# Products of queries and keys laid out element by element for the sum on TensorE

## The reference

```
xn = layernorm(x)
q = xn @ Wq + bq                      # (B, T, 16 heads, 8)
kv = (xn @ Wdown + bdown) @ Wup + bup # (B, T, 16 heads, 16)
k, v = split(kv)
att = einsum('bthd,btgd->bthg', q, k) / sqrt(8)
att = softmax(att)
out = einsum('bthg,btgd->bthd', att, v) @ Wout + bout
x = x + out + moe0(xn)                # 8 experts, top 2
x = x + hyena(layernorm(x)) + moe1(layernorm(x))
```

## Time and profile before

| | us |
|---|---|
| median of 3 runs | 1367.02 |
| lowest and highest | 1363.98, 1368.1 |
| the profiled execution | 1364.03 |
| its span, first to last instruction | 1362.1 |
| TensorE matmuls busy | 1123.0 (82%) |
| VectorE busy | 831.2 (61%) |
| GpSimd busy | 796.9 (59%) |
| ScalarE busy | 596.3 (44%) |
| mean granted TensorE clock | 0.954 |

### The profile page before, as it was taken

How to read it: one execution, slowest core, us unless ns; L and a number is a source line. 1 busy time by engine, 2 the same in 40 slices (tenths; PEclk the granted TensorE clock), 3 DMA queues, 4 the chain that set the end, 5 groups by cost and what they waited for, 6 DMA issues and landing times.

```text
span 1362.1 us, 19492 instructions
## 1 busy us (share of the span) xinstructions
PE 1123.0 (82%) x6608; PEld 873.0 (64%) x6608; DVE 831.2 (61%) x1139; ACT 596.3 (44%) x1529; POOL 796.9 (59%) x613
## 2 busy tenths in 40 slices
PE   1448999999998988988783458899869999999975
PEld 1432222223887776777672457799868899899965
DVE  7946999997999999999998975111121000000038
ACT  0120011112766566656564448800005666656667
POOL 4605877873889899989881004767533445445520
PEclk9998999999999999999995779999989999999988
DMA  5471332131454554554445420199995767777747
GB/s 174 161 298 64 112 115 111 51 102 33 143 165 145 155 147 147 162 150 152 136 130 196 155 92 30 53 296 327 317 338 145 204 203 202 205 204 202 203 187 216
DMA packets 119955, 225.63 MB, mean 166 GB/s; under 512 B 16709, under 2 KB 80101, under 8 KB 117810
## 3 DMA queue, kind: packets, MB, share of 16 engines
q1 hardware_dynamic: 102164, 188.16, 44.9%
q0 software_dynamic: 17344, 35.57, 7.2%
q10 hardware_dynamic: 350, 0.67, 0.2%
HBM read 157.19 MB, written 67.14 MB: 165 GB/s over the span
## 4 chain that ended last, share of the span: by engine, by line
PE 42%; POOL 24%; DVE 11%; DMA 10%; ACT 6%; issue 6%; SPq 1%; POOLq 0%; ACTq 0%; DVEq 0%
PE ps L721 14%; POOL BG L259 12%; POOL y_tok L429 12%; PE ps L679 9%; PE ps L692 9%; DMA TPB<-in_kpad 5%; DVE XN L893 3%; DMA FF<-sorted_x 2%; PE ps L803 2%; DVE stats L863 2%; PE ps L805 2%; PE ps L668 1%; PE ps L730 1%; DMA xt_d<-xT 1%; DVE X L1037 1%
## 5 line engine op out<-in xcount | busy, mean ns | idle before, releaser
L429 POOL DMA_INDIRECT y_tok<-FF,yidx x284 | 306.9, 1081 | 206.0 <-ACT FF L497 146.0
L421 POOL DMA_INDIRECT sorted_x<-XN,idx x256 | 278.8, 1089 | 90.1 <-issue 89.0
L692 PE MATMUL ps<-FF 128*128 128x128 f32 x2272 | 278.8, 276 | 0.0
L692 PEld LDWEIGHTS ps<-FF 128*128 128x128 f32 x2272 | 266.9, 193 | 14.4 <-issue 4.3
L679 PE MATMUL ps<-FF 128*128 128x256 f32 x1136 | 273.8, 385 | 0.0
L488 ACT ACTIVATE FF<-ps,FF 128x256 f32<-128x256 f32 x568 | 230.2, 481 | 34.0 <-PE ps L679 33.1
L679 PEld LDWEIGHTS ps<-FF 128*128 128x128 f32 x1136 | 208.5, 194 | 23.3
L721 PE MATMUL ps<-BG,cst 128*128 128x512 f32 x208 | 193.3, 1097 | 0.0
L1146 DVE TENSOR_TENSOR BG<-BG,ps 128x512 f32<-128x512 f32 x16 | 10.6, 686 | 290.6 <-PE ps L837 290.4
L259 POOL TENSOR_TENSOR BG<-TPB 128x2048 f32<-128x2048 f32 x38 | 171.6, 4515 | 25.6 <-DVE BG L1028 13.6
L1016 DVE TENSOR_TENSOR BG<-BG,TPB 128x1024 f32<-128x1024 f32 x128 | 147.8, 1215 | 0.0
(11 more groups left out here) (185 smaller groups left out, 1676.7 us busy)
## 6 DMA issues: line engine op xcount, KB each, us to landing
FF<-in_moe SPq DMA_DIRECT2D x142, 514.0 KB
TPB<-in_kpad SPq DMA_DIRECT2D x22, 1024.0 KB, 7.8
sorted_x<-TPB SPq DMA_DIRECT2D x36, 516.0 KB, 4.1
FF<-sorted_x SPq DMA_DIRECT2D x142, 129.0 KB
FF<-in_kpad SPq DMA_DIRECT2D x10, 1024.0 KB
BG<-y_tok SPq DMA_DIRECT2D x8, 1024.0 KB, 6.6
X<-y_tok SPq DMA_DIRECT2D x8, 1024.0 KB, 6.5
y_tok<-FF,yidx POOLq DMA_INDIRECT x284, 3.2
```

The costliest lines, as they stand in the source:

```text
L421: pool.indirect_dma_start(sorted_x[layer], bass.IndirectOffsetOnAxis(ap=idx[:, k, j:j + 1], axis=0), XN[:, j, :], None).then_inc(s_sc, 16)
L429: pool.indirect_dma_start(y_d[layer], bass.IndirectOffsetOnAxis(ap=yidx[:, G % 4, r:r + 1], axis=0), ys[:, G % 4, r * D:(r + 1) * D], None ...
L692: t = pe.matmul(psY[:, r * P:(r + 1) * P], hT[:, G % 2, m, r * P:(r + 1) * P], wc[:, G % 4, HID + m * D:HID + (m + 1) * D], start=False, s ...
```

## The change

For the first 13 pairs the layout of `qkv` for queries and keys changes from head by head (16 heads of 8 elements) to element by element (8 elements, each with 16 heads). The evacuation on ScalarE, which was one copy of 384 columns, becomes a copy of 256 that regroups queries and keys as it reads them from PSUM, and a plain copy of 128 for the values. `own_product` on VectorE still takes 4 instructions of 1024 elements a pair, each over 4 elements, 16 heads and 16 heads. In them the query is repeated along the innermost dimension, and the key along the middle one. `prod` then holds, for each element, the 256 scores of a tile side by side. The matmuls of `sum_products` read two runs of 256 floats, one of each tile; their count, size and accumulation are the same. Pairs 13 to 31 keep their layout and their code, and no wait is added or removed.

```diff
@@ evac_qkv, ScalarE
-                act.copy(qkv[:, m % 4, t, :], bank[:, 0:3 * D]).then_inc(s_qkv, 1)
+                if m < OWN:
+                    act.copy(qkv[:, m % 4, t, 0:2 * D].rearrange("p (a e h) -> p a e h", a=2, e=DH),
+                             bank[:, 0:2 * D].rearrange("p (a h e) -> p a e h", a=2, e=DH))
+                    act.copy(qkv[:, m % 4, t, 2 * D:3 * D], bank[:, 2 * D:3 * D]).then_inc(s_qkv, 1)
+                else:
+                    act.copy(qkv[:, m % 4, t, :], bank[:, 0:3 * D]).then_inc(s_qkv, 1)
@@ sum_products, TensorE
-                pr = prod[:, b % 2, :].rearrange("p (n e) -> p e n", e=DH)
+                pr = prod[:, b % 2, :].rearrange("p (t e n) -> p e t n", t=2, e=DH)
                 for e in range(DH):
-                    t = pe.matmul(psS[b % 2][:, :], ident, pr[:, e, :], start=(e == 0), stop=(e == DH - 1))
+                    t = pe.matmul(psS[b % 2][:, :].rearrange("p (t n) -> p t n", t=2), ident, pr[:, e, :, :],
+                                  start=(e == 0), stop=(e == DH - 1))
@@ own_product, VectorE
                 dve.wait_ge(s_qkv, 2 * b + 2)
+                n = DH // 2
                 for t in range(2):
-                    for h0 in (0, H // 2):
-                        i = qk_product(dve, b, t, h0, H // 2)
+                    for e0 in (0, n):
+                        q = qkv[:, b % 4, t, e0 * H:(e0 + n) * H].rearrange("p (e h) -> p e h", e=n)
+                        k = qkv[:, b % 4, t, D + e0 * H:D + (e0 + n) * H].rearrange("p (e g) -> p e g", e=n)
+                        o = t * 2048 + e0 * H * H
+                        i = dve.tensor_tensor(
+                            prod[:, b % 2, o:o + n * H * H].rearrange("p (e h g) -> p e h g", e=n, h=H),
+                            q[:, :, :, None].to_broadcast([P, n, H, H]), k[:, :, None, :].to_broadcast([P, n, H, H]),
+                            ALU.mult)
```

## The result

The changed kernel took 1351.62 us (median of four, 1349.03 to 1351.73), the kernel before, timed beside it, 1365.5 us (1362.06 to 1368.1). The ratio is 0.9891, with a 95% interval of 0.9871 to 0.9912: 1.1% faster. The forecast was 1355.8 with 1351 to 1362. Applied to the 1367.02 us of before, the ratio gives 1352.1. The profiled execution took 1351.53 us, its span 1349.4, against 1364.03 and 1362.1.

The account below looks back on a forecast made before the run. TensorE's strided sum held back the first expert tile, with GpSimd's scatter and row loads next. First tile -12.6 us, cold start +1.4, sum -11.2 from 1367.02: 1355.8 us, range 1351 to 1362.

Parts of the forecast that it names:

- the stride is the price: On TensorE, line 721's read of every eighth float makes blocks slow; reading neighbours takes 6.9 us in place of 14.7.
- the steady step: VectorE's step falls from 17.98 to 16.42 us, with no wait for the sum.
- a sign of being wrong: Wrong if the first expert tile starts before 319 or after 327 us, or the product line's mean leaves 1.22 us.
- The gathered copy: ScalarE's evacuations of pair 0, ahead of the first scatter, cost +0.8 us (0.3 to 1.8).
- The extra group in the scatter: With a faster VectorE, one more group of four two-input products falls within GpSimd's scatter: +1.4 us.
- the prediction's alternative: By the skill's page, the extra group costs GpSimd's scatter nothing and the sum is 1.4 us better.
- The row loads' landing: From row loads issued (318.0) to the first expert transposition (321.5): 3.5 us, taken from layer 1.
- the cold start: TensorE begins the expert tiles after a rest, at a lower clock: +1.4 us (bound +3).
- 1 (no shrinking): TensorE's block stays over 13 us and the copy's cost adds 5.8 us: 1372.8 us; chance 0.05.
- 2 (a dear repeated read): VectorE's repeated innermost read is dear; at double the price 1393 us; chance 0.02.
- 3 (the scatter suffers more): GpSimd's scatter excess grows by a fifth, 6 us later: 1361.5 us; chance 0.12 with other hand-over losses.
- 4 (the clock falls): TensorE's rests drop its clock to 1.2 GHz; at four fifths of the time there, 1372.6 us; chance 0.05.

Follow-up runs that it names:

- slow_vector: Kernel after with one more VectorE reduction of 0.68 us behind each of the 12 products of pairs 1 to 12: 1357.83 us, ratio 0.9939.
- no_reduce: Kernel after without VectorE's sums of the weighted values for the first twelve pairs, a memset in their place: 1358.81 us.
- the delay: Eight GpSimd memsets, each waiting for the one before, ahead of the first scatter: kernel before 1367.43 us, ratio 0.9996; kernel after 1356.89 us, ratio 0.9923.
- the earlier routing: VectorE's product of pair 0 moved behind the routing work: kernel before 1375.61 us, ratio 1.0058; kernel after 1343.6 us, ratio 0.9831.

## Why the prediction was right in direction and short in size

**What held.** That the stride is the price (a block of 7.1 us at the full clock, 6.9 forecast, and mostly 8.8 at the clock it got), that VectorE's products stay at 1.22 us, the steady step (16.36 us, 16.4 forecast) with no wait for the sum, the scores of pair 12 (304.67, 305.2 forecast), that the last scatter and the row loads take the block's place, that TensorE starts from rest (4.61 us from the first to the third transposition in place of 3.15: +1.46, forecast +1.4), and that the phase behind moves as a whole (the product of pair 14 by 15.85 us, layer 1's first tile by 15.86).

**What failed is the size: -12.6 us at the first tile measured -17.3.** The prediction named a first tile before 319 us as a sign of being wrong, and it came at 316.77. The step that failed is the path from the first scatter to the first tile: when the scatter starts, what it loses, and how long its rows take to land. Four terms make the 4.7 us:

- *The gathered copy.* +0.8 us at the first scatter, from 0.62 us for 256 gathered floats; it measured 0.373, less than what the plain price of the earlier trace rows gives (0.17 + 256 x 0.81 ns = 0.38), and the second copy 0.271. A tile costs 0.16 us more, and the first scatter came at 112.73, 0.4 earlier than before; over the runs with this routing order it stood between 112.7 and 113.7. 1.2 us of the miss. I had taken the price from line 601, which gathers from SBUF in steps of 64 floats, and set it against line 470, a plain read of PSUM. The copy here gathers from PSUM in steps of eight. Which of the two, memory or step, makes line 601 dear no run shows. The Trainium skill's rule of 8-byte cachelines (page "PSUM — Partial Sum Buffer", section "Specifications (TRN2)") speaks of matmuls; for ScalarE's read of PSUM these rows show no such price. The rows of ScalarE, source view (ns min/median/max, first and last start, forms):

```profile
L504 ACT COPY TPB<-ps x26: 372/373/373, 86.5 to 274.8; 128x256 f32<-128x256 f32 x26
...
L506 ACT COPY TPB<-ps x26: 271/271/272, 86.7 to 275.1; 128x128 f32<-128x128 f32 x26
```

- *The extra group in the scatter.* Forecast +1.4, measured -0.2 (32.8 against 33.0 us over 0.96 each). This step was wrong in kind: a group has no fixed price. Two more groups fell into the scatter (24 in place of 22), but each cost 1.37 us instead of 1.50, since the scatters met them at other offsets. That the two cancel is chance, and so the prediction's alternative, an extra group that costs nothing, has the right number for no reason of its own. The 128 scatters of the runs with the same products spread from 153.9 to 159.8 us. 1.6 us.
- *The gaps within the scatter*, which the sum did not have: the idle time between scatters fell from 43.1 to 41.8 us, the copy between the two halves waits 2.9 us instead of 1.4 for its DMA but takes 0.57 instead of 1.25. Together 0.4 to 0.5 us less.
- *The row loads' landing.* 3.5 us, taken from layer 1, measured 1.98 (314.79 to 316.77). In every run of this study where the tiles wait for the scatter, the first tile comes 3.3 to 3.5 us behind its end, where the sum had 4.8. 1.5 us.

The wait that ends last, the scatter and the landing of its rows, was right, and so was the path behind it; the terms on it were mis-sized, and the one for the extra group had its mechanism wrong. With the measured values in their place the sum gives 1355.8 - 4.7 = 1351.1 us.

**The sum against the time.** The first tile's 17.3 less 1.5 for the cold start are 15.8, and 15.9 arrive at layer 1. The expert stage of layer 1 then lasted 294.0 us instead of 290.8, so that the span shows 12.7. Over all runs this stage took 289.8 to 295.6 us with no relation to the edit, so I take it as that stage's own spread. It is luck that it hid 3.2 of the 4.7 us in the profiled execution. The median moved by 13.9 us against the kernel before, timed beside it.

**The rivals.** 1 (no shrinking) did not occur. 2 (a dear repeated read) did not. Its room for VectorE, "1 us each before anything is lost", was wrong as a statement: slow_vector added 0.68 us a step and the last scatter ended 4.4 us later (1.0 of it at its start). 3 (the scatter suffers more) did not occur in the changed kernel but did in two experiments (+4.1 us busy in slow_vector, +8.0 in no_reduce); the loss is real, but goes by the offsets and not by how dense VectorE's work is. 4 (the clock falls) did occur: the granted clock was 1.00, 0.68 and 0.89 in three windows of 16 us,

```profile
174.00:190.00 16.00, 9.84 (x29) 4.55 (x29) 15.93 (x16) 2.08 (x6) 12.79 (x11) 1.00 0.33 121
190.00:206.00 16.00, 13.16 (x27) 6.05 (x28) 15.93 (x16) 1.54 (x4) 12.81 (x11) 0.68 0.33 120
206.00:222.00 16.00, 12.28 (x32) 5.39 (x31) 15.96 (x15) 2.23 (x7) 10.64 (x10) 0.89 0.29 108
```

against 1.00 in the busy steps of before. The 10.2 us of a step at the worst of them are 10.2 / 0.68 = 15.0, still less than VectorE's 16.4, and TensorE's busy time in these rows is 9.8 to 13.2 us of 16. The rival's mechanism was there and its price was not, in the steady steps. (That rival's arithmetic counts shares of the work, 10.2 x 1.8 = 18.4 us; for four fifths of the time at the lower level it would be 10.2 / 0.6 = 17.0.) The lower clock cost one wait of 4.05 us in the second step, where 0.8 was forecast, and that lies ahead of VectorE's slack and off the path.

## What to carry to other kernels

When a bound is removed, price what stands next as carefully as the bound itself: here the gain was set by a scatter's end and a load's landing, and all of the error lay there. An edit that costs nothing, or hurts, while something else is last (the delay and the earlier routing in the kernel before) has another sign once it is gone; try such edits again after each change of the bound. Where two engines hold each other up, look at the offset at which their instructions meet before giving a group a fixed price: less work on one of them can move the offset for the worse. Take an engine's read price from the same memory and the same step, and read a chain that runs through 0.3 us of idle time with a look at whether there is a wait in the code at all.

## What the runs showed of the hardware that I had not expected

- TensorE's fp32 moving read nearly keeps its rate two floats apart (7.47 us a block against 7.03), and halves it at four (14.75), with nothing more lost at eight (14.85).
- ScalarE's gathered read of 256 floats from PSUM, in steps of eight floats, costs what a plain one does (373 ns, and 370 for the plain copy of 256 on line 497 of the kernel before). Its gathered read of SBUF in steps of 64 floats costs 1.076 us for 512, while the exponential of line 512 reads 512 adjacent floats of SBUF in 0.632.
- The GpSimd instruction that issues a scatter is held up by a VectorE product with two SBUF inputs in which it starts: it ends 0.83 us after the product does, up to 1.97 us in all instead of 0.96. Beside reductions it takes 0.96. Taking reductions out made the first tile 6.7 us later, since the offsets changed. The Trainium skill, page "SBUF — State Buffer", section "Who interferes with whom", infers that such a product does not hold descriptor writing up. The instruction that issues the descriptors is held up here; whether in writing them or in reading its offsets from SBUF, no run separates.
